# The last result rows of a mixture-of-experts layer: fewer products, sums on other engines, another order of slots

## The reference, cut to what matters

```python
# x: [1250, 512]; 64 experts, each 512 -> 256 -> 512; 2 experts per token
sel = _route(xn, hash_proj, 2)                     # [1250, 2]
pos = running count of earlier choices of the same expert
buf[expert, pos] = xn[token]
h   = gelu(buf @ W1[expert]); y = h @ W2[expert]
out = x + mean over k of y[sel[t, k], pos[t, k]]
```

## Time and profile before

| | us |
|---|---|
| median of 3 runs | 568.66 (568.55, 568.66, 571.02) |
| profiled execution | 566.68 |
| its span, first to last instruction | 564.9 |

### The profile page before, as it was taken

How to read it: one execution, slowest core, us unless ns; L and a number is a source line. 1 busy time by engine, 2 the same in 40 slices (tenths; PEclk the granted TensorE clock), 3 DMA queues, 4 the chain that set the end, 5 groups by cost and what they waited for, 6 DMA issues and landing times.

```text
span 564.9 us, 8479 instructions
## 1 busy us (share of the span) xinstructions
PE 528.3 (94%) x2789; PEld 366.1 (65%) x2791; DVE 347.5 (62%) x978; ACT 253.0 (45%) x534; POOL 95.0 (17%) x123
## 2 busy tenths in 40 slices
PE   0799999999989999999999999998899999999797
PEld 0344444455479888799999999985455455544455
DVE  4888787776976455548886233596335344344667
ACT  2787766666445534046664222442443343433300
POOL 4141111100000000000000000004334445445400
PEclk9999999999999999999999999999999999999999
DMA  8500000000020008293009212699999999999668
GB/s 303 201 2 1 1 1 1 1 1 0 2 76 0 1 1 278 95 321 117 2 1 343 79 63 76 270 404 341 347 403 416 411 417 411 414 414 413 280 261 318
DMA packets 32409, 105.70 MB, mean 187 GB/s; under 512 B 5040, under 2 KB 10417, under 8 KB 25324
## 3 DMA queue, kind: packets, MB, share of 16 engines
q1 hardware_dynamic: 22364, 86.09, 39.2%
q0 software_dynamic: 4880, 9.78, 4.7%
q10 hardware_dynamic: 5120, 9.26, 4.6%
HBM read 93.49 MB, written 17.84 MB: 197 GB/s over the span
## 4 chain that ended last, share of the span: by engine, by line
PE 76%; DMA 11%; DVE 7%; issue 3%; SPq 2%; DVEq 1%; ACT 0%; POOLq 0%
PE PS L533 8%; PE PS L532 8%; PE PS L534 8%; PE PS L816 6%; DMA BIG<-in_we 6%; PE PS L607 6%; PE PS L830 6%; PE PS L570 5%; PE PS L562 5%; PE PS L636 4%; PE PS L637 4%; PE PS L753 3%; PE PS L596 3%; DMA BIG<-xx_rows,TIDX 2%; SPq L1584 2%
## 5 line engine op out<-in xcount | busy, mean ns | idle before, releaser
L532 PE MATMUL PS<-ROUND 128*128 128x416 f32 (+3 forms) x232 | 83.9, 361 | 0.0
L533 PE MATMUL PS<-ROUND 128*128 128x416 f32 (+3 forms) x232 | 83.6, 360 | 0.0
L534 PE MATMUL PS<-ROUND 128*128 128x416 f32 (+3 forms) x232 | 83.4, 359 | 0.0
L830 PE MATMUL PS<-BIG 128*64 128x512 f32 x208 | 52.9, 592 | 0.2 <-DVE BIG L1233 0.2
L1067 DVE BATCH_NORM_STATS2 BST<-BIG 128x6 f32<-128x416 f32 (+1 forms) x36 | 20.7, 590 | 44.3 <-ACT BIG L1411 35.7
L636 PE MATMUL PS<-ROUND 128*128 128x416 f32 (+3 forms) x120 | 43.5, 363 | 2.3 <-DVE ROUND L984 1.8
L532 PEld LDWEIGHTS PS<-ROUND 128*128 128x128 f32 (+1 forms) x232 | 43.5, 188 | 2.6
L534 PEld LDWEIGHTS PS<-ROUND 128*128 128x128 f32 (+1 forms) x232 | 43.6, 188 | 2.5
L966 DVE TENSOR_TENSOR BIG<-PS,BIG 128x280 f32 (+17 forms) x69 | 30.7, 445 | 23.5 <-PE PS L596 19.6
L533 PEld LDWEIGHTS PS<-ROUND 128*128 128x128 f32 (+1 forms) x232 | 43.5, 188 | 2.3
L947 DVE TENSOR_SCALAR BIG<-BIG 128x180 f16<-128x180 f16 (+20 forms) x157 | 43.1, 321 | 0.0
(11 more groups left out here) (268 smaller groups left out, 971.7 us busy)
## 6 DMA issues: line engine op xcount, KB each, us to landing
BIG<-in_we SPq DMA_DIRECT2D x46, 1024.0 KB
BIG<-in_we SPq DMA_DIRECT2D x12, 512.0 KB
y_rows<-KVB SPq DMA_DIRECT2D x19, 256.0 KB
BIG<-y_rows SPq DMA_DIRECT2D x9, 512.0 KB, 7.5
EXTRA<-in_we SPq DMA_DIRECT2D x4, 1024.0 KB
XA<-in_we SPq DMA_DIRECT2D x4, 1024.0 KB
BIG<-in_wqkvp ACTq DMA_DIRECT2D x3, 1024.0 KB, 14.6
XA<-in_we SPq DMA_DIRECT2D x6, 512.0 KB
```

The lines of the kernel that those rows point to most:

```text
L532: mm(o, ah, bh, start=first, stop=False)
L533: mm(o, ah, bl, start=False, stop=False)
L534: return mm(o, al, bh, start=False, stop=last)
L830: ins = mm(PS[64 * j:64 * j + 64, b, :], HT[:, s, 128 * f2 + 64 * j:128 * f2 + 64 * j + 64], weights(2 * r + j, 1024 + 512 * f2, 512), sta ...
```

## The change

Four things change together.

1. *Pair 29 is scattered for some tiles.* With `FIRST_OF_LAST = 6`, pair 29 goes to `y_rows` for the tokens of tiles 6 to 9 and through products for those of tiles 0 to 5. Its scatter uses `SCL`, a copy of its indices in which those below 6 * 256 are moved out of bounds; its HOT has 1000 columns in place of 1250. SP loads tiles 0 to 5 as before, then waits for pair 29's scatter, and loads tiles 6 to 9. PE makes six products for tiles 0 to 5 and four for tiles 6 to 9: 52 in place of 60.
2. *Evictions and splits are parted.* All pairs' "down" steps now stand where `expert_order` has them; the splits of pairs 29, 30, 31 are steps of their own, behind the next pair's "hid" copy. `NM2` is made while pair 28 is evicted.
3. *Sums move.* For tiles 2, 4, 6 and 8 ACT takes off the shift (an activation with a bias, between its stores), POOL adds the second row, and VectorE does only the finish.
4. *Slots are spread.* `IOTAQ` gives four neighbouring partitions the positions m, m+16, m+32, m+48 (and for one half of them m+40 downwards in the third place), so that the filled slots are strewn over the 64 partitions of an expert in place of filling the first ones.

The core of the diff:

```diff
+FIRST_OF_LAST = 6
+STEPS = [FIRST_OF_LAST] + [NT] * (LATE - 1)
+ON_POOL = (2, 4, 6, 8)
...
     order = expert_order()
-    for r in range(32 - LATE, 31):
-        order.remove(("down", r))
-        order.insert(order.index(("hid", r + 1)) + 1, ("down", r))
+    for r in range(32 - LATE, 32):
+        order.insert(order.index(("hid", r + 1)) + 1 if r < 31 else len(order), ("split", r))
...
-                        for t in ts:
-                            if t == 0 and j < 8:
+                        begin = min(t for t in range(LATE) if j < STEPS[t])
+                        for t in ts:
+                            if t < begin:
+                                continue
...
-            V.tensor_copy(IOTAQ[:, 0:64], IOTA[:, 0:64])
-            V.tensor_scalar(IOTAQ[:, 64:128], IOTA[:, 64:128], -1.0, 63.0, ALU.mult, ALU.add)
+            spot = IOTAQ[:, 0:64].rearrange("p (b m a) -> p b m a", b=2, m=8)
+            link(V.tensor_copy(spot, IOTA[:, 0:64].rearrange("p (a b m) -> p b m a", a=4, b=2)))
+            link(V.tensor_scalar(spot[:, 1, :, 2], IOTA[:, 40:48], -1.0, 87.0, ALU.mult, ALU.add))
+            V.tensor_scalar(IOTAQ[:, 64:128], IOTAQ[:, 0:64], -1.0, -1.0, ALU.mult, ALU.add)
...
+                    if r == 30 - 2 * LATE:
+                        link(V.tensor_copy(SCF[:, 0:1], SCIDX[:, 32 - LATE:33 - LATE]))
+                        link(V.tensor_scalar(SCF[:, 1:2], SCF[:, 0:1], 256.0 * FIRST_OF_LAST - 0.5, 8192.0, ALU.is_lt, ALU.mult))
+                        V.tensor_tensor(SCL, SCF[:, 0:1], SCF[:, 1:2], ALU.add).then_inc(s_scl, 1)
...
+                    if r == 31 - LATE:
+                        dve.wait_ge(s_nm, NT)
+                        V.tensor_scalar(NM2, NM[:, :], -2.0, None, ALU.mult).then_inc(s_nm2, 1)
+                elif kind == "split":
+                    t = r - (32 - LATE)
+                    dve.wait_ge(moved[b], use)
+                    link(V.tensor_scalar(YHI[:, t, :], YS[r % NY], 0.5, None, ALU.mult))
+                    V.scalar_tensor_tensor(YLO[:, t, :], YS[r % NY], 0.5, YHI.bitcast(F32)[:, t, :], ALU.mult,
+                                           ALU.subtract).then_inc(s_split, 1)
...
+                if i + 2 in ON_POOL:
+                    m = rows(i + 2)
+                    act.wait_ge(sd_row[i + 2], 32)
+                    A.activation(YL[0:m, i + 2, 0, :], YL[0:m, i + 2, 0, :], ACT.Identity,
+                                 bias=NM2[0:m, i + 2:i + 3]).then_inc(s_ymid, 1)
                 act.wait_ge(s_res, 1 + i + 1)
                 act.dma_start(out[128 * i:128 * i + n, :], YL[0:n, i, 0, :]).then_inc(sd_out, 16)
...
+            for q, i in enumerate(ON_POOL):
+                n = rows(i)
+                pool.wait_ge(s_ymid, q + 1)
+                G.tensor_tensor(YL[0:n, i, 0, :], YL[0:n, i, 0, :], YL[0:n, i, 1, :], ALU.add).then_inc(s_ysum, 1)
...
-            for sm, value in stored(sd_ys, 31 - LATE, NY):
-                sp.wait_ge(sm, value)
             for i in range(NT):
                 n = rows(i)
+                if i in (0, FIRST_OF_LAST):
+                    for sm, value in stored(sd_ys, 31 - LATE + (i > 0), NY):
+                        sp.wait_ge(sm, value)
```

More of the change, by code:

```diff
@@ L429, in gnn_mix_moe @@
         YL = big(20240, 10240).rearrange("p (i a d) -> p i a d", i=NT, a=2)
-        HOT = by(rounded(KK0, 1250 * LATE), LATE)
+        WIDE = [-(-min(128 * t, N) // 250) for t in STEPS]
+        HOT = [rounded(KK0 + 250 * sum(WIDE[:t]), 250 * WIDE[t]) for t in range(LATE)]
         YHI, YLO = (by(rounded(36992 + 512 * LATE * q, 512 * LATE), LATE) for q in range(2))
         LTK, LTQ = big(32800, LATE), by(big(32800 + LATE, 5 * LATE), LATE)
+        SCL, SCF = big(32800 + 6 * LATE, 1).bitcast(I32), big(32801 + 6 * LATE, 2)
         yv = y_d.rearrange("(t a) d -> t a d", a=2)
@@ L484, in gnn_mix_moe @@
                              "agg", "hth", "htl", "qz", "qzl", "kvt", "mh"))
-        s_hot, s_xz, s_nwt = sem("hot"), sem("xz"), sem("nwt")
+        s_hot, s_xz, s_nwt, s_split, s_scl, s_nm2, s_ymid, s_ysum = (
+            sem(n) for n in ("hot", "xz", "nwt", "split", "scl", "nm2", "ymid", "ysum"))
         (s_link, s_w1h, s_w1s, s_w2s, s_nv, s_ns, s_nb, s_relu, s_h1h, s_h1s, s_xst, s_rstd, s_nm, s_sel, s_par, s_lgz, s_ohs, s_lq,
@@ L513, in stored @@
             return [(sems[q % n], 16 * (q // n + 1)) for q in range(max(0, last - n + 1), last + 1)]
-        LAST = [(31 - LATE - q) // NY + 1 for q in range(NY)]
+        LAST = [(32 - LATE - q) // NY + 1 for q in range(NY)]
         def conv_free(j):
@@ L526, in end_of_experts @@
             eng.wait_ge(full[b], use)
-            for sm, value in stored(sd_ys, 31 - LATE, NY):
+            for sm, value in stored(sd_ys, 32 - LATE, NY):
                 eng.wait_ge(sm, value)
@@ L842, in tensor @@
                         n, (b, use) = rows(j), at_of(("fin", j))
+                        begin = min(t for t in range(LATE) if j < STEPS[t])
                         for t in ts:
-                            if t == 0 and j < 8:
+                            if t < begin:
+                                continue
+                            if t == begin and j < 8:
                                 pe.wait_ge(moved[b], use - 1)
-                            elif t == 0:
+                            elif t == begin:
                                 pe.wait_ge(s_res, 1 + j - 8 + 1)
@@ L849, in tensor @@
                                 pe.wait_ge(s_hot, t + 1)
-                                bd, ud = at_of(("down", 32 - LATE + t))
-                                pe.wait_ge(moved[bd], ud)
-                            mm(PS[0:n, b, :], HOT[:, t, 128 * j:128 * j + n], YHI[:, t, :], start=(t == 0), stop=False)
-                            ins = mm(PS[0:n, b, :], HOT[:, t, 128 * j:128 * j + n], YLO[:, t, :], start=False,
+                                pe.wait_ge(s_split, t + 1)
+                            mm(PS[0:n, b, :], HOT[t][:, 128 * j:128 * j + n], YHI[:, t, :], start=(t == begin), stop=False)
+                            ins = mm(PS[0:n, b, :], HOT[t][:, 128 * j:128 * j + n], YLO[:, t, :], start=False,
                                      stop=(t == LATE - 1))
@@ L1226, in vector @@
             for step in eviction_order():
-                kind, r, (b, use) = step[0], step[1], at_of(step)
+                kind, r, (b, use) = step[0], step[1], at_of(("down", step[1]) if step[0] == "split" else step)
                 if kind == "hid":
@@ L1262, in vector @@
                 full_dve(dve)
-            dve.wait_ge(s_nm, NT)
-            link(V.tensor_scalar(NM2, NM[:, :], -2.0, None, ALU.mult))
+            dve.wait_ge(s_nm2, 1)
             for i in range(NT + 1):
-                if i < NT:
+                if i < NT and i not in ON_POOL:
                     n = rows(i)
@@ L1276, in vector @@
                     dve.wait_ge(full[b], use)
-                    dve.wait_ge(s_link, done[0] - (1 if i < NT else 0))
+                    if i - 1 in ON_POOL:
+                        dve.wait_ge(s_ysum, ON_POOL.index(i - 1) + 1)
+                    else:
+                        dve.wait_ge(s_link, done[0] - (1 if i < NT and i not in ON_POOL else 0))
                     V.scalar_tensor_tensor(y, y, 0.5, PS[0:n, b, :], ALU.mult, ALU.add).then_inc(s_res, 1)
@@ L1572, in gpsimd @@
                     gather_pair(r + NX)
-                if r != 1 and r - 1 <= 31 - LATE:
+                if r != 1 and r - 1 <= 32 - LATE:
                     scatter_pair(max(r - 1, 0))
```

22 lines of the change are left out of this document (10 added, 12 removed).

## The result

The changed kernel takes 565.57 us (median of 20 runs, 562.22 to 575.29) against 568.63 for the kernel before (median of 20, 565.39 to 574.98). The ratio is 0.9948 with a 95% interval of 0.9930 to 0.9967. Some executions are over 1.5% longer than the fastest of the same kernel (three of the changed kernel's 20); medians in this document hold them, ratios leave them out. The forecast was 565.1.

The account below looks back on a forecast made before the run. PE was taken as the bound up to about 518 us, then the transfers; 2.2 us before pair 31's second products, 1.2 in the tail and 0.1 for gathers make 3.5, from 568.66 to 565.1 us, range 562.2 to 568.0.

Parts of the forecast that it names:

- Spread slots: Weight transfers of the last pairs: evened over engines, PE's 3.4 us of weight waits go, gather's wait 1.3 to 0.9.
- Rival 1: Last pairs: the spreading does nothing, weight waits stay, the tail gives 1.2 to 1.7: 567.6 us; chance 0.17.
- In the new order each moves 5: Expert transfers: each engine moves 5 filled slots of an expert, where before some moved 8 and others only 4.
- What is late next: Pairs 28 to 31: PE waits 1.3 us for pair 30's gelu; pair 31's second products start at 542.2.
- D: Start of pair 31's second products on PE: forecast 542.5, which is 2.2 us earlier than before (544.73).
- Evictions ahead of copies: Pair 31: pair 30's eviction now precedes the hidden-row copy PE waits for, costing 0.3 us (between 0 and 0.69).
- The tail: From pair 31's second products to the last finish: 16.1 us in place of 17.3, a gain of 1.2.
- PE's pause stays: Tail: PE's pause for pair 31's split, taken as 0.4 us, remains as before.
- Loads of tiles 6 to 9: SP's loads after pair 29's scatter, landed by 544.5: tile 9's rows come by 556.8, needed at 556.2; costed at nothing.
- Rival 3: SP's wait before tile 6: a late scatter of pair 29 delays tile 9's rows, slower, 569.7 us; chance 0.05.
- Sum: Whole kernel: 2.2 + 1.2 + 0.1 for gathers is 3.5 us, taken from 568.66: 565.1 us.
- the 0.62 for a clear gain: Whole run: probability 0.62 of being faster by more than 0.5%, 2.8 us; same had 0.31, slower 0.07.

Follow-up runs that it names:

- the four orders: The changed kernel with its spread slots (ratio 0.9948), with the old order (1.0019), reversed within groups of four (1.0015), or filled slots crowded together (1.0108).
- hot_early: The changed kernel with SCL, LTQ and the HOT matrices made after the hidden-row copies of pairs 26, 27 and 28: 566.93 us, ratio 0.9964.
- no_pool: The changed kernel with all ten sums on VectorE, none on GpSimd: 565.37 us, ratio 0.9959.
- no_spread: The changed kernel with the old order of slots, the rest of the change kept: 569.28 us, ratio 1.0019.
- combo_pass: The kernel of combo with ScalarE's pass for tiles 3, 5 and 7 made ahead of a store: 563.96 us, ratio 0.9937.
- fill24: The changed kernel with 24 filler products in place of 20 before the first gather's wait: 564.17 us, ratio 0.9932.
- all_ten: The changed kernel with all ten tiles taking three pairs by products, 60 products in place of 52: 566.11 us, ratio 0.9950.
- crowded: The changed kernel with filled slots crowded on as few groups of four partitions (and those 32 higher) as can be: 573.58 us, ratio 1.0108.
- combo: The changed kernel with 24 fillers, HOT matrices after the copies, and sums of tiles 3, 5, 7 on ScalarE and GpSimd: 562.70 us, ratio 0.9915.
- swap_in_fours: The changed kernel with the old slot order, reversed within each group of four neighbouring partitions: 570.17 us, ratio 1.0015.

## Why the prediction was right, and where it was off

**Spread slots: right.** The share stays at 1.00 to 532 and drops to 0.25, the two weight waits are gone, and the four orders differ as the mechanism says. Rival 1 falls. By the ratios the spreading is worth 0.34% put into the kernel before (1.9 us) and 0.7% taken out of the changed one (4 us). Both are more than half of the gain, but the first has an interval of 0.01% to 0.67%, so its share is not sharp. "In the new order each moves 5" is nearly so: with 39 rows seven groups have 5 and one has 4.

**What is late next: right in kind, D 1.0 us too early.** Forecast 542.5, measured 543.52. The 4.99 us from eviction to gelu held exactly; both came about 1 us late, the eviction at 532.74 in place of 531.6 and the gelu at 537.73 in place of 536.75. The terms: pair 28 started at 523.92 in place of 523.5, in an execution that had lost 1.7 us to the clock in front. PE waited 1.06 us for pair 30's gelu (forecast 1.3), and the gather's wait was 1.22 (forecast 0.9, before 1.3), so in this execution fewer packets on the fullest engine did not bring it forward. What I had not counted are pair 28's second products, which stood 0.49 us for the copy of hidden rows behind a HOT matrix, so that pair 30 started 5.11 after pair 29. The small instructions for `SCL` held the copy of pair 26 as well: pair 27 starts 4.57 after pair 26 in place of 4.40. The step counted HOT only where the root stood behind it, not where a copy did. hot_early showed that all of this is VectorE's order: without it pair 28 to D is 17.60.

**Evictions ahead of copies: right.** From pair 31's first products to D it is 4.83 us, against 4.60 before; forecast 0.3, measured 0.23.

**The tail: the step that failed in size.** Forecast D + 16.1, measured D + 16.84. "PE's pause stays" was wrong: the products on both sides of it start 1.04 us apart in place of 0.39, so it is 0.65 longer, because GpSimd's add of tile 2 ran beside the split, whose first half took 1.07. The sum of tile 9 took 1.20 beside the add of tile 8, which itself ended at D + 15.10, 0.6 later than forecast. The sentence on the Trainium skill, page "SBUF — State Buffer", section "Who interferes with whom", named this exclusion, with an end of D + 16.4. I had weighed it only at tile 9 and had not looked at what stands beside the first add. With both, 16.1 + 0.3 for the sum and up to 0.65 for the pause come to 16.4 to 17.05. The trace bears out the rule against the sum that I took, and no_pool has the same end with no sum on GpSimd at all.

**Loads of tiles 6 to 9: right that they cost nothing, but later than forecast.** The first loads began at 537.39, earlier than the 539.6 forecast, 3.2 us after pair 28's scatter was issued and not 6.5. Pair 29's took 7.3 us (539.15 to 546.41), so the load of tile 6 was issued at 546.48; "issued by 544" was missed by 2.5 us. SP waited 6.0 us for that scatter, and nobody waited for the loads:

```profile
SPq L1708 <- DMA y_rows<-BIG: 6.0, 1, 6.0
```

The share from 538 to 558 us, by stretches of 2 us, never fell below 0.84. Rival 3 was near all the same: in no_spread tile 9's rows held the end for 1.31 us, and in combo_pass for 0.15.

**Sum: the number was right partly by luck.** 565.1 against 565.57 looks closer than the terms are. The forecast was made from a profiled execution 2.0 us below its median. The one after stands 0.5 below its own and holds the clock's fall. Counting only distances from pair 28 on, the change gives 1.25 before D and 0.43 behind it, 1.7 in place of the 3.4 forecast (whose 2.2 for D held 0.4 ahead of pair 28). The other 1.4 us of the medians' 3.06 lie before pair 28 or between executions. Counted from the first pair's products to the last finish, it is 164.82 us before and 163.63 in the changed kernel, 161.95 without the 1.68 of the clock: 2.9 less, of which 1.2 lie before pair 28. One profile each can't say whose they are: from pair 3 to pair 25, where PE's pace is 4.40 us a pair, before has three longer distances (4.78, 4.72 and 5.62, together 1.92 more) and the changed one two (4.52 and 4.92, 0.64 more), so some of it may be the spreading too. That isn't shown: no_spread's first 28 pairs, less its 3.9 us at the lower clock, are as short (125.7 us against 125.5).

The gain of 3.06 us stands just above the 2.8 us under which the prediction can't tell a difference from none, and its interval (0.33% to 0.70%) holds that line. So the 0.62 for a clear gain is neither borne out nor refuted.

## What to carry to other kernels

Rows that are scattered or gathered by an indirect transfer should be laid over the partitions so that every group of four, and the one 32 higher, holds the same number of filled ones; look at how steeply the DMA share falls at the end of a stream to see whether it is needed. Before an elementwise step goes to GpSimd, list what VectorE does in those 1.3 us: here, beside instructions that read only SBUF, four moved sums won nothing. And where a wait goes away, look at every instruction that had hidden behind it, the small copies too.

## What was not expected of the hardware

While GpSimd adds two SBUF tiles (1.29 us), a VectorE instruction with SBUF operands alone stands, and it ends a fixed time behind the add. For the split's first half, which has a single input, that was 0.28 to 0.29 us in five kernels (changed, fill24, all_ten, hot_early, crowded). For two inputs, sums and once the split's second half, it was 0.55 or 0.56 in 24 places in ten kernels. A finish, which reads PSUM and SBUF, kept its 0.69 us beside the same add (549.64 in combo, with the add from 549.52 to 550.81). I had looked for two inputs alone. The same section of the Trainium skill also says that a one-input `tensor_scalar` can run in a mode that takes both port pairs and then shuts GpSimd out or is shut out, by whichever issues first. The trace agrees where the add is first, with 0.42 us alone and up to 1.28 beside the add. The other order came twice. In no_spread VectorE's sum began 0.18 us before the add, and the add took 1.72 us in place of 1.29. In swap_in_fours the split's first half began 0.23 us before it, kept its 0.43, and the add took 1.34.

At the first pair a wait of PE of 2.00 to 3.68 us for the gather went with a halved clock in all six profiles that had one. The pair's products then took 3.43 to 3.68 us in place of 1.95, so it costs 1.5 us at least; in no_spread the second pair's took 3.62 as well. The length of the wait doesn't decide it alone. For pair 30's weights PE waited 2.23 us in the kernel before and the clock stayed at 1.00; it waited 2.19 us in crowded and 2.44 in swap_in_fours and the clock fell. What decides it stays open.
